# Routing and experts in one block, with weight parts among the lists and 62 tiles of softmax inside the second attention

## What is computed

```python
x = x + o @ Wout.T                          # end of the second attention
tok = x.reshape(-1, d)                      # 8192 tokens
gate = jax.nn.softmax(tok @ Wgate.T, axis=-1)
k_cap = bs // E                             # 1024
vals, idx = jax.lax.top_k(gate.T, k_cap)    # each expert's 1024 best tokens
g = _ln(tok[idx_flat], mlp_g, mlp_b)
y = gelu(einsum('ked,ehd->keh', g, fc1s) + b1s)
y = einsum('keh,edh->ked', y, fc2s) + b2s
tok = tok.at[idx_flat].add(y * w)           # w = vals
```

## Times and profile before

| | us |
|---|---|
| median of 3 runs (2446.69 to 2448.96) | 2448.49 |
| the profiled execution | 2448.41 |
| its span | 2446.6 |
| TensorE busy in the span | 2316.8 |
| DVE busy | 1906.6 |
| ACT busy | 1548.6 |
| POOL busy | 1031.7 |
| first weight matrix of an expert, issue to landing (median) | 4.9 |
| second weight matrix of an expert, issue to landing (median) | 7.0 |

### The profile page before, as it was taken

One profiled execution on the slowest core, in us unless ns is written; L12 is line 12 of the kernel. 1 busy time (PEld: TensorE's weight loads), 2 busy tenths in 40 slices (PEclk: granted clock), 3 DMA queues, 4 the chain that ended last, 5 costly groups with the idle time before them and its releaser, 6 DMA issues. The chain is left out here.

```text
span 2446.6 us, 67114 instructions
## 1 busy us (share of the span) xinstructions
PE 2316.8 (95%) x24912; PEld 2059.0 (84%) x24912; DVE 1906.6 (78%) x3763; ACT 1548.6 (63%) x2982; POOL 1031.7 (42%) x939
## 2 busy tenths in 40 slices
PE   7999999999999899999999999999999727999997
PEld 6888888899999788888888888888888626999996
DVE  8999999667666788888888888888888686666663
ACT  6999998766666556555565656565656454656653
POOL 5888888200000244434343434343444203445544
PEclk9999999999999899999999999999999856999998
DMA  4111110101101000000000000000000022334423
GB/s 145 44 39 42 43 39 25 55 23 32 32 22 33 27 19 13 17 13 17 13 17 13 17 15 15 17 13 17 13 17 13 29 46 71 88 96 87 96 53 35
DMA packets 78720, 89.21 MB, mean 36 GB/s; under 512 B 18480, under 2 KB 72496, under 8 KB 76080
## 3 DMA queue, kind: packets, MB, share of 16 engines
q1 hardware_dynamic: 66352, 71.10, 9.4%
q0 software_dynamic: 12288, 17.05, 4.3%
HBM read 62.42 MB, written 25.69 MB: 36 GB/s over the span
## 5 line engine op out<-in xcount | busy, mean ns | idle before, releaser
L1276 POOL TENSOR_TENSOR a_rq<-a_vq,minus_half 128x8 f32<-128x8 f32 x256 | 417.7, 1641 | 97.0 <-DVE a_vq L1300 97.0
L1223 ACT ACTIVATE a_sq<-a_bqk 128x512 f32<-128x512 f32 x256 | 152.8, 597 | 350.7 <-PE a_bqk L126 347.4
L1271 POOL TENSOR_TENSOR a_rstd<-a_veps,minus_half 128x1 f32<-128x1 f32 x63 | 34.8, 553 | 580.3 <-DVE a_veps L1347 580.3
L124 PE MATMUL a_bqk<-wqk_hi,a_h_lo 128*128 128x512 f32 x512 | 207.6, 406 | 3.5 <-DVE a_h_lo L1316 3.5
L126 PE MATMUL a_bqk<-wqk_hi,a_h_hi 128*128 128x512 f32 x512 | 201.2, 393 | 0.0
L125 PE MATMUL a_bqk<-wqk_lo,a_h_hi 128*128 128x512 f32 x512 | 201.0, 393 | 0.0
L1292 DVE TENSOR_TENSOR a_qk<-a_bqk,a_rq 128x512 f32<-128x512 f32 x256 | 176.0, 688 | 29.6 <-POOL a_rq L1276 29.5
L1208 ACT COPY a_vs<-a_ba 64x512 f32<-64x512 f32 x256 | 148.8, 581 | 53.5 <-PE a_ba L126 48.9
L1902 ACT ACTIVATE e_u<-e_bu,e_b 128x512 f32<-128x512 f32 x128 | 88.2, 689 | 149.2 <-PE e_bu L126 146.2
L2044 DVE TENSOR_TENSOR e_u_lo<-e_u,e_u_hi 128x512 fp32r<-128x512 f32 x128 | 88.5, 691 | 119.5 <-ACT e_u_hi L1907 116.9
L1284 DVE TENSOR_REDUCE a_ss<-a_sq 128x8 f32<-128x512 f32 x256 | 173.9, 679 | 2.1 <-ACT a_sq L1223 0.8
(11 more groups left out here) (329 smaller groups left out, 8031.5 us busy)
## 6 DMA issues: line engine op xcount, KB each, us to landing
a_qk<-gates_of_rows SPq DMA_DIRECT2D x32, 256.0 KB, 4.3
tokens<-a_xs SPq DMA_DIRECT2D x64, 128.0 KB, 1.7
out<-a_xs SPq DMA_DIRECT2D x64, 128.0 KB, 1.7
e_w<-in_fc1s SPq DMA_DIRECT2D x8, 1024.0 KB, 4.9
e_w<-in_fc2s SPq DMA_DIRECT2D x8, 1024.0 KB, 7.0
a_gate<-gates_of_rows SPq DMA_DIRECT2D x122, 64.0 KB, 2.5
X<-in_x SPq DMA_DIRECT2D x56, 128.0 KB, 2.1
wst<-in_qkv_w SPq DMA_DIRECT2D x16, 128.0 KB, 2.5
```

The source lines that it names most:

```text
L124: tensor.matmul(to, w_lo, x_hi, start=start, stop=False)
L1223: nc.scalar.activation(sq[:, n * BK:(n + 1) * BK], b_qk[:, n * BK:(n + 1) * BK], ACT.Square).then_inc(s["sq"], 1)
L1276: nc.gpsimd.tensor_tensor(rq[:, 8 * n:8 * n + 8], vq[:, 8 * n:8 * n + 8], g.mhalf[:, 0:8], ALU.pow).then_inc(s["rq"], 1)
```

## The change

Three parts.

1. Softmax over experts is divided. For the 62 tiles whose scores are there when attention reaches step 64 (`EARLY = NT - 2`), the six operations run inside that step, in place in `g.lg`, with three unused stretches of `a_qk` for maximum, sum and reciprocal. Routing does the same six on the last two tiles. Everything after reads `g.lg`.
2. Routing and experts run in one block. The barrier and the clearing between them are gone; in their place TensorE waits for all row writes, POOL's later gathers wait for the row writes of their expert, and all buffers that both phases need at once are allocated outside of them (`pair` shares memory with `e_u`, which is first written later). The semaphores of both are cleared at the end of the kernel.
3. Work for the first expert is moved among the lists: ACT makes the four high weight parts behind `pair` 3 to 6, DVE does the moments of the first 512 rows and one low part between the last two row writes. DVE's second low part and its first one for the second matrix come behind the first normalisation. On POOL the first root comes ahead of the gathers for the third pass.

The core of the diff. The three places in attention stand behind ACT's copies into `PT`, behind DVE's product with `rs`, and behind DVE's `o_lo`; the two in routing's list loop stand behind `pair` on ACT and behind the row write on DVE. In `program` the other four engines are joined as SP is. The bodies of both phases are otherwise only indented differently:

```diff
+EARLY = NT - 2
...
+        early = g.lg[:, :, 0:EARLY]
+        emx, esm, ers = (qk[:, n * NT:n * NT + EARLY] for n in range(3))
...
@@ attention1_phase, scalar @@
+                if has(-1) and not has(0):
+                    act.wait_ge(s["prob"], 2)
+                    nc.scalar.activation(early, early, ACT.Exp).then_inc(s["prob"], 1)
...
@@ attention1_phase, vector @@
+                if has(-1) and not has(0):
+                    dve.wait_ge(s["lg_out"], EARLY)
+                    nc.vector.reduce_max(emx, early.rearrange("p e t -> p t e"), AX).then_inc(s["prob"], 1)
+                    dve.wait_ge(s["prob"], 1)
+                    nc.vector.tensor_tensor(early, early, emx.unsqueeze(1).to_broadcast([P, E, EARLY]),
+                                            ALU.subtract).then_inc(s["prob"], 1)
...
+                if has(-1) and not has(0):
+                    dve.wait_ge(s["prob"], 3)
+                    nc.vector.reduce_sum(esm, early.rearrange("p e t -> p t e"), AX).then_inc(s["prob"], 1)
+                    dve.wait_ge(s["prob"], 4)
+                    nc.vector.reciprocal(ers, esm).then_inc(s["prob"], 1)
+                    dve.wait_ge(s["prob"], 5)
+                    nc.vector.tensor_tensor(early, early, ers.unsqueeze(1).to_broadcast([P, E, EARLY]), ALU.mult)\
+                        .then_inc(s["prob"], 1)
...
@@ route_phase, scalar @@
+                    if e == 3:
+                        act.wait_ge(s["saved"], 16)
+                    if 3 <= e < 7:
+                        experts.weights_ahead(act, e - 3)
...
@@ route_phase, vector @@
+                if e == E:
+                    experts.rows_ahead(dve)
...
@@ experts_phase @@
+        def weights_ahead(act, n):
+            if n == 0:
+                act.wait_ge(g.loaded_e, 80)
+            (high_w1 if n < 2 else high_w2)(act, 0, n % 2)
+
+        def rows_ahead(dve):
+            dve.wait_ge(g.loaded_e, 80)
+            moments(dve, 0)
+            low_w1(dve, 0, 0)
...
@@ experts_phase, gpsimd @@
+            root(0)
+            gather(2)
+            root(1)
...
@@ experts_phase, vector @@
+            normal(0)
+            low_w1(dve, 0, 1)
+            low_w2(0, 0)
+            split_h(0)
+            low_w2(0, 1)
+            moments(dve, 1)
...
@@ experts_phase, tensor @@
             pe.wait_ge(g.loaded_e, 80)
+            pe.wait_ge(g.rows_out, 2 * E)
             pipeline_by(2, pe, step, E, 1, 1)
...
-        m.clear()
+        return EnginePrograms(m.sems, sync, scalar, gpsimd, vector, tensor)
...
@@ program @@
-            route_phase(nc, a, g)
-            experts_phase(nc, a, out, g)
+        experts = experts_phase(nc, a, out, g)
+        route = route_phase(nc, a, g, experts)
+        with whole, nc.Block() as block:
+            @block.sync
+            def _(sp):
+                route.sync(sp)
+                experts.sync(sp)
...
+        m.sems += route.sems + experts.sems
+        m.clear()
```

More of the change, by code:

```diff
@@ new lines, in gpsimd @@
+        def gpsimd(pool):
+            nc.gpsimd.memset(ones[:, :], 1.0).then_inc(s["consts1"], 1)
+            nc.gpsimd.tensor_tensor(low[:, :], cst[:, C_UP:C_UP + P], cst[:, C_SAME:C_SAME + P], ALU.mult)\
+                .then_inc(s["consts1"], 1)
+            pool.wait_ge(s["saved"], 16)
+            pool.wait_ge(s["rows_out"], 2)
+            pool.sem_inc(s["held"], 1)
+            for h in range(2):
+                for k in range(GT):
+                    c = h * GT + k
+                    nc.gpsimd.indirect_dma_start(
+                        g.xg[h][:, k, :], None, g.tok_dram.rearrange("t p d -> (t p) d"),
+                        bass.IndirectOffsetOnAxis(g.rows[:, 0, c:c + 1], 0)).then_inc(g.gathered[h], 16)
@@ new lines, in tensor, with step @@
+        def tensor(pe):
+            pe.wait_ge(s["prob"], 1)
+            for b in range(4):
+                last = nc.tensor.transpose(b_t[:, b * P:(b + 1) * P], pb[:, :, :].rearrange("p e t -> p (e t)").rearrange("p (k b) -> p b k", b=4)[:, b, :],
+                                           cst[:, C_ID:C_ID + P])
+            last.then_inc(s["tr"], 1)
+            for i in range(2 * STAGE):
+                pe.wait_ge(s["same"], 1)
+                pe.wait_ge(s["count"], 2 * (i + 1))
+                pe.wait_ge(s["count_a"], 2 * (i + 1))
+                if i:
+                    pe.wait_ge(s["digit"], i)
+                nc.tensor.matmul(b_n[:, 0:RADIX - 1], same[:, :], cnt[:, :], start=True, stop=True)\
+                    .then_inc(s["counted"], 1)
+            pe.wait_ge(s["consts1"], 2)
+            pe.wait_ge(s["scan"], 1)
+            nc.tensor.matmul(b_g[:, 0:1], low[:, :], inc_g[:, TB - 1:TB], start=True, stop=True).then_inc(s["pre"], 1)
+            nc.tensor.matmul(b_e[:, 0:1], cst[:, C_SAME:C_SAME + P], inc_g[:, TB - 1:TB], start=True, stop=False)
+            pe.wait_ge(s["scan"], 2)
+            nc.tensor.matmul(b_e[:, 0:1], low[:, :], inc_e[:, TB - 1:TB], start=False, stop=True).then_inc(s["pre"], 1)
+            pe.wait_ge(s["place"], 3)
+            for b in range(4):
+                last = nc.tensor.transpose(b_t[:, b * P:(b + 1) * P], place[:, b * P:(b + 1) * P], cst[:, C_ID:C_ID + P])
+            last.then_inc(s["turned"], 1)
+            def step(e, has, par):
+                if has(0):
+                    pe.wait_ge(s["hot_hi"], e + 1)
+                    pe.wait_ge(s["pair"], e + 1)
+                    pe.wait_ge(s["pair_p"], e + 1)
+                    if later(e) and later(e - 1):
+                        pe.wait_ge(s["rows_out"], 2 * (e - 1))
+                    for t in range(NT):
+                        last = nc.tensor.matmul(b_l[par][0:RH, 0:2 * RL], hot_hi[:, par, t // 2, :, t % 2],
+                                                pair[:, par, t // 2, :, t % 2], start=(t == 0), stop=(t == NT - 1))
+                    last.then_inc(s["lists"], 1)
+            pipeline_by(2, pe, step, E, 0, 2)
```

917 lines of the change are left out of this document (435 added, 482 removed).

## The result

| | before | after |
|---|---|---|
| median us (5 runs each) | 2448.49 (2446.57 to 2448.96) | 2435.84 (2433.92 to 2436.37) |
| the profiled execution | 2448.41 | 2433.92 |
| its span | 2446.6 | 2432.2 |

The ratio is 0.9947, with a 95% interval of 0.9936 to 0.9957: 12.65 us less, by the medians.

The account below looks back on a forecast made before the run. TensorE was taken to bound the kernel except in the hole from routing to the first expert matmul, so gains there count fully. 2448.41 - (3.6 + 8.95 = 12.55) = 2435.9 us, range 2433 to 2440.5.

Parts of the forecast that it names:

- The opening: Start of routing: six softmax operations on 2 tiles instead of 64 save 3.6 us (3.1 to 3.7).
- Covers at no cost: Attention's end and the list loop: the moved softmax and weight work fits in idle engine time, costing nothing.
- Rival (a): List loop: ACT's high parts make tile copies late in four turns, adding 4.2 us, 2440.1; chance 0.07.
- Barrier, moments and root: Last row write to first normalisation: start moves from 2052.36 to 2043.4, saving 8.95 us (8.7 to 9.2).
- A mere slowdown to 1.50: POOL's first root: it only runs slower beside DVE's low part, ending at 2042.9; the alternative not taken.
- The clock: Experts' start: TensorE's half-speed stretch of 4.9 us costs 2.4 us now; change in this cost taken as zero.
- the range's 0.9 us for an earlier rise: Experts' start: a clock rise after 3 us instead of 4.9 would save 0.9 us, put in the range.
- the 1.5 us at the upper end: Experts' start: a clock rise after 8 us instead of 4.9 would cost 1.5 us, put in the range.
- rival (b): Experts' start: the clock rises only after 10 us, costing 2.5 us, 2438.4; chance 0.07.
- (c): All 128 expert steps: moved buffer addresses slow the matmuls, 2441 at 2% and 2454 at 5%; chance 0.04.
- (d): Experts' entry: something other than barrier and gathers holds it, only the front's 3.6 us comes, 2444.9; chance 0.04.
- The sum: Whole kernel: 3.6 + 8.95 = 12.55 us saved, giving 2435.9 us.

Follow-up runs that it names:

- late_softmax: Changed kernel with only 2 softmax tiles in attention's end and 62 left in routing; median 2437.8 us, ratio 0.9962 to the kernel before.
- three_copies: Changed kernel with each of the four high weight parts among the lists made three times on ACT; one profiled run, 2435.71 us.
- moments_only: Changed kernel with high parts behind the lists and first low part behind the first normalisation, only the moments still ahead; median 2434.21 us, ratio 0.9946.
- low_behind: Changed kernel with only the first low part moved behind the first normalisation, high parts left among the lists; one profiled run, 2438.0 us.
- gathers_first: Changed kernel with POOL's four gathers ahead of the first root, as in the kernel before; median 2435.2 us, ratio 0.9954.
- before_root_first: Kernel before with one edit, POOL's first root issued ahead of its four gathers; median 2446.72 us, ratio 0.9993.
- rows_behind: Changed kernel with first moments and first low part behind the last row write again, high parts still among the lists; median 2438.41 us, ratio 0.9960.
- both_behind: Changed kernel with first moments and low part behind the last row write and the four high parts behind the lists; median 2438.9 us, ratio 0.9971.
- warm: Changed kernel plus unused TensorE matmuls, 4 before and 8 behind the first transposes, ahead of the first expert matmul; one profiled run, 2438.93 us.
- other_offset: Changed kernel with padding ahead of the experts' weight parts at 56 elements instead of 40, moving buffers by 64 bytes; median 2436.5 us, ratio 0.9953.

## Why the prediction was right, point by point

**The opening: 3.6 us said, 3.53 measured.** The small operations are 0.17 to 0.18 us, as in the rows taken. late_softmax returns it.

**Covers at no cost: right.** The residual sum still has idle time ahead of it, and the row writes kept their 3.90 us. The cover among the lists was argued from too narrow a gap; it held with more to spare (three_copies). Rival (a)'s 4.2 us was priced wrongly too: even three parts a turn cost 1.5.

**Barrier, moments and root: 8.95 us said; 8.88 at the normalisation, 8.77 at the first matmul.** The root did wait for the low part: it ended 0.90 us behind that part's end, 1.94 us in all, and 1.03 us with no subtraction beside it (moments_only, low_behind). A mere slowdown to 1.50 is out. The missing 0.1 us is the normalisation beside POOL's gathers, 1.50 in place of 1.39 us. The Trainium skill, "SBUF — State Buffer", section "SBUF: two separate sides", has a DVE operation with two SBUF inputs and a GpSimd operation that reads SBUF exclude each other for the whole instruction. The waiting root agrees with it (1.94 against 1.03 us).

**The account of this term was loose.** The prediction put the root's place ahead of the gathers beside the end of the barrier as what frees the path. gathers_first shows that the order is worth nothing once there is one block; before_root_first that it is worth 1.0 us in the kernel before. What counts is that the moments, with the low part beside the root, run before the last row write: 3.7 of the 8.8 us (rows_behind). The other 5.0 are gained even with everything behind the row write (16.70 to 11.66, both_behind), and they have a part that the prediction never named: DVE's order. In the kernel before, the moments stand behind the first low part, and that waits for ACT's first high part; in both_behind they come first. The rows divide the 5.0: 1.8 us from the row write's end to the first operation behind the barrier (2043.09 to 2044.89), 1.15 until the high part releases DVE (2046.04), 1.14 for the low part (moments at 2047.18), and 1.0 for the gathers ahead of the root (before_root_first). This is an estimate from the rows of two traces; only the last part was tried alone. The prediction's sum held because it went by where the normalisation stood and where it would stand, not by what each step is worth. And the first low part ahead of the last row write takes 0.24 us away, since the root waits for it.

**The clock: zero said, 0.2 us of gain measured, and the reasoning was wrong.** I reckoned 0.47 us for each microsecond at the lower level. But TensorE waits 0.77 to 0.88 us for the second normalisation in both kernels, and that comes from DVE and POOL, whatever the clock. In rows_behind, twelve matmuls at the lower level ended only 0.27 us ahead of the transposes and their distance was even shorter (5.73). warm shows it from the other side. So the range's 0.9 us for an earlier rise was not there to be had. A later rise is another matter: the lower level costs nothing only up to the second transposes, 5.7 to 6.1 us behind the first matmul. Behind them nothing hides it, and in warm, where it lasted there from about 2055.1 to 2058.5, the stretch was 1.5 us longer. How much of the 1.5 us at the upper end and of rival (b)'s 2.5 would have come is not shown; by this reckoning it is less than was said, since the part ahead of the transposes is free.

**Rivals (c) and (d)** did not occur: passes keep their pace, and the entry moved whole. other_offset speaks against (c) at one more address. The time given for (c) at 2% was a slip: 0.057 us in 128 steps is 7.3 us, so 2443 and not 2441.

**A term left out: the end of the kernel.** The prediction put nothing there; the stretch behind the last scatter's start is 0.46 us longer (9.57 to 10.03).

**The sum: 12.55 us said, 12.49 by distance, 12.65 by the medians.** The nearness is partly luck. The entry gave 0.2 us less than said at the first matmul, the second transposes came 0.2 earlier, and the 0.46 at the end of the kernel was not counted: 12.0 us with it. That the median came out at 2435.84 against 2435.9 is better than the scatter warrants: the five runs of the changed kernel alone spread over 2.4 us.

## What to carry to other kernels

An operation's length on the chain that ended last is not what its removal gives: the four gathers took 5.6 us there and were worth 1.0 alone; ask for each what stands ready behind it, and name the last operation that needs nothing new (here the moments). Work is hidden in a loop as long as the helper engine's whole turn stays under the bounding engine's turn, which can be more than the gap that is seen. TensorE's lower clock costs only where nothing else is late; here, warming it up paid only together with removing the next wait, and alone it made the kernel slower inside the trace.

## What the runs showed of the hardware that was not expected

A wait of 2.96 us on TensorE, at full clock, was followed by matmuls at the lower level (0.43 us apart, window mean 0.68) in warm. The clock rose after differing times in kernels with the same instructions at that place. In attention's end the mean is 0.88 in the window of before (16.8 to 18.8 us behind the last softmax's maximum) and 0.55 in the one of after (16.6 to 18.6 behind it). At the experts' start it rose about 4.4 us behind the first expert matmul in the changed kernel, and only after the twelve matmuls in rows_behind, over 5.4 us behind the first (2047.41; mean 0.50 in the window 2052 to 2053, 0.75 in the next). A POOL operation that starts beside a DVE subtraction of two inputs is delayed to its end and more: 1.94 us for 1.03 beside one of 1.22 us, while the subtraction keeps its 1.22.
